# Layer norms moved into the attention stages, first projection weights loaded before the stage that uses them

## The chip, the cores and the metric

The kernel runs on one core of a Trainium2 chip. The metric is device time in microseconds (us), median of three runs.

## The reference, cut to what matters

All arithmetic is float32; x is 16 sequences of 256 tokens and 128 channels.

```python
x = layernorm(x + attention_0(x))      # 16 heads of 8, relative position tables
x = layernorm(x + ffn_0(x))            # itself 6 layers: local attention (16 heads of 64, window 32)
                                       #   and a gated FFN, each with its own residual
x = layernorm(x + attention_1(x))      # 16 heads of 8, causal, over 16 x 256 tokens
x = layernorm(x + moe(x))              # 8 experts, top 2
def layernorm(x): return (x - mean(x)) / sqrt(var(x) + 1e-5)   # over the 128 channels
```

`attention_0` is softmax((q.k + relative terms) / sqrt(8)) times (v + relative values). `ffn_0` multiplies x by Wqkv (128 x 3072) in every layer, normalises and rotates q and k, takes a softmax over a window of 32 keys back, and multiplies by Wo (1024 x 128).

## The kernel before, in words

x lies in SBUF for the whole program as `X` (128 partitions, 32 tiles of 128 channels; a sequence is two tiles). `XR` is a second tensor of that shape. Nothing is scheduled automatically: each engine has a queue that is written out by hand, runs it in order, and waits on semaphores. The program is a row of blocks; an engine enters a block when all have left the one before.

- **Stage A, first attention** (L222 to L898). PE, ScalarE (ACT), VectorE (DVE) and GpSimd (POOL) each run `sequence("first")`, `sequence("loop")` for 15 sequences and `sequence("last")`. PE's products go through a ring of two PSUM banks (`ring_plan`, L99) that ACT and DVE free. DVE writes four groups of outputs per sequence into `XR`; SyncE (SP) stores each with 16 DMAs to a DRAM buffer `oa` (`stores`, L876 to L884), which changes their layout. `q_blk` holds blocks of the queries, which PE reads in `relative_keys`.
- **ln1** (`layer_norm`, L903 to L977). One DMA brings `oa` back into `XR` (L919). DVE adds it to X, takes `bn_stats` and `bn_aggr` over 8 tiles at a time, POOL raises the variance to -0.5 (L968), DVE scales X (L953) and ACT copies X to `XR` (L977), since the residual of the 6-layer part is needed later.
- **Stage B, the 6-layer FFN** (L984 to L1864). A small block loads the rotation tables and masks and lets POOL clear buffers (L1077 to L1102). Then ACT loads Wqkv (1.5 MB, L1577) and splits it in a high part (`high_parts`, L1585) and POOL in a low part (`low_part`, L1235). SP fetches a sequence of X into `xcur` (`fetch_x`, L1202), POOL splits it (`split_x`, L1267 and L1270). Per sequence and layer there are 4 steps; in each PE projects, ACT squares (L1609), DVE rotates (`rotate`, L1740 to L1742), and POOL adds, takes the power and scales (`normalise_rows`, L1241, L1245, L1250). The steps are software pipelined: `one_pass("first")` fills the pipeline, `one_pass("loop")` runs it. SP also copies the values of every step into windows (`windows`, L1149 to L1153).
- **ln2** is `layer_norm` again, without the load and the copy.
- **Stage C, second attention** (L1869 to L2273). A small block loads weights with 14 DMAs, and DVE spreads and scales them (L1916 to L1924). POOL copies a sequence into `xcur` (L1981), PE transposes and projects (L2019), 8 slots per sequence follow, with row maxima on DVE (L2213) and exponentials on ACT (L2169).
- **Stage D, experts** (L2290 on). SP loads the weights with 8 DMAs. The third norm runs per group of 8 tiles: `statistics3` on DVE, `scales3` on POOL, `normalise3` on ACT; PE transposes X (L2404) and computes the gates (L2413).

The 16 stores of a group are issued as

```python
for h in range(8):
    for x in range(2):
        row = 64 * (h // 4) + 32 * x + h % 4 * HD
        sp.dma_start(oa[...], yout[row:row + HD, b * 4 + g, :]...).then_inc(oa_st, 16)
```

Of the kernel before, what the change touches and what calls it, by code (L numbers as in the profile page):

```python
# [25 lines left out]
P = 128  # L26
# [102 lines left out]
def build_program(nc, T, out):  # L129
    ctx = ExitStack()  # L130
    with ctx:
# [27 lines left out]

        x_in = T["L0_attn_x"].rearrange("b (t p) c -> p (b t) c", p=P)  # L160
# [3 lines left out]
        with ExitStack() as st:  # L164
# [21 lines left out]
            q_blk, k_blk = (sb(st, n, [P, H, S]) for n in ("a_q_blk", "a_k_blk"))  # L186
# [13 lines left out]
            yout = XR[:, :, :].rearrange("p t (a c) -> p (t a) c", a=2)  # L200
# [21 lines left out]
            with nc.Block() as block:  # L222
# [119 lines left out]
                def _(pe):  # L342
# [8 lines left out]
                    for i in range(6):  # L351
# [29 lines left out]
            rsum_ok, ysum_ok, yout_ok, oa_st = (sem("a_rsum_ok"), sem("a_ysum_ok"), sem("a_yout_ok"),  # L381
                                                sem("a_oa_st"))
# [7 lines left out]
            with nc.Block() as block:  # L390
                @block.gpsimd
                def _(pool):
                    def sequence(part, b):
# [32 lines left out]
                    with pool.Fori(0, B - 1) as b:  # L426
                        sequence("loop", b)
# [236 lines left out]
                def _(act):  # L664
                    def sequence(part, b):
# [75 lines left out]
                    with act.Fori(0, B - 1) as b:  # L741
                        sequence("loop", b)
                    sequence("last", B - 1)

                @block.vector
                def _(dve):
# [4 lines left out]
                    def sequence(part, b):  # L751
# [85 lines left out]
                        if ahead:  # L837
                            low_parts(qs, q_next, q_low)
                            low_parts(ks, k_parts, k_low)
# [25 lines left out]
                    with dve.Fori(0, B - 1) as b:  # L865
                        sequence("loop", b)
                    sequence("last", B - 1)

                @block.sync
                def _(sp):  # L870
# [5 lines left out]
                    def stores(b, g):  # L876
                        lt, hh = g // 2, g % 2
                        sp.wait_ge(yout_ok, b * 4 + g + 1)
                        for h in range(8):
                            for x in range(2):  # L880
                                row = 64 * (h // 4) + 32 * x + h % 4 * HD
                                sp.dma_start(
                                    oa[b, lt, :, HD * x:HD * x + HD, hh, h, :].rearrange("k l d -> l k d"),
                                    yout[row:row + HD, b * 4 + g, :].rearrange("p (k d) -> p k d", d=HD)  # L884
                                ).then_inc(oa_st, 16)

                    next_x(1)
                    with sp.Fori(0, B - 2) as b:
                        stores(b, 0)
                        stores(b, 1)  # L890
                        next_x(b + 2)
                        stores(b, 2)
                        stores(b, 3)
                    for b in range(B - 2, B):
                        for g in range(4):
                            stores(b, g)

                    sp.wait_ge(oa_st, 16 * B * 4 * 16)  # L898


        def layer_norm(tag, residual, load=None, keep=None, store=None):
            GT = 8
            with ExitStack() as st:  # L903
                stats = sb(st, f"{tag}_stats", [P, 2, GT, 6])
                mv = sb(st, f"{tag}_mv", [P, 2, GT, 2])
                var = sb(st, f"{tag}_var", [P, 2, GT])
# [962 lines left out]
        with ExitStack() as st:  # L1869
# [55 lines left out]

            CS = 4 * LT
# [743 lines left out]
```

## Time and profile before

| | us |
|---|---|
| median of 3 runs | 5302.65 (5301.96 to 5303.74) |
| profiled execution, its own time | 5298.32 |
| its span, first to last instruction | 5296.5 |
| PE busy | 4807.8 (91%) |
| POOL busy | 3431.2 (65%) |
| DVE busy | 3833.2 (72%) |
| ACT busy | 3250.9 (61%) |

The shares are averages over stages with different limits. The program runs stage A to about 1139 us of the span, stage B from 1187 to 4486, stage C from 4510 to 5146 and stage D to the end; the norms lie between. Busy time says nothing of waits, so the stretches between the stages are read from the timeline, which lists instructions in order of time with the idle time of the engine in front of them and what ended it.

### The profile page before, as it was taken

Reading aid. Unit: us, or ns where it says so; the run is one execution under the profiler, and the core shown is the slowest. Engines: PE = TensorE matmul, PEld = TensorE weight load, DVE = VectorE, ACT = ScalarE, POOL = GpSimd, SP = SyncE. Lnnn points to the kernel's source line nnn. Section 1 sums busy time; section 2 is a strip of 40 time slices with the busy share of each in tenths; the row PEclk is TensorE's granted clock in tenths of the full one; section 3 lists DMA queues with packets and bytes.
Section 4 is the critical chain, followed back from the end, with each engine's and each line's share of the span. In section 5 each row is a group of like instructions: output and inputs, shape, how many; then the busy total and the mean of one; then the engine's idle time right before and its main releaser. Section 6 shows DMA issues by size and latency. Waiting matters only on the chain. (4 is left out here: it accounts for less than half of the span.)

```text
span 5296.5 us, 207054 instructions
## 1 busy us (share of the span) xinstructions
PE 4807.8 (91%) x84978; PEld 3972.3 (75%) x84978; DVE 3833.2 (72%) x7728; ACT 3250.9 (61%) x6115; POOL 3431.2 (65%) x2197
## 2 busy tenths in 40 slices
PE   6999999958999999999999999999999997688879
PEld 4888888846887788877887788778877885455557
DVE  4777777756887788877887788778877886444543
ACT  2333333326777777777777777777777774466654
POOL 1111111119999999999999999999999995211212
PEclk8999999988999999999999999999999998888889
DMA  1000000013222322232222322232222221000000
GB/s 44 6 6 6 6 6 6 6 31 87 69 69 67 86 70 68 69 85 69 68 68 72 83 68 68 70 83 68 68 71 72 68 68 38 4 0 0 0 5 17
DMA packets 418744, 253.85 MB, mean 48 GB/s; under 512 B 200864, under 2 KB 414398, under 8 KB 417487
## 3 DMA queue, kind: packets, MB, share of 16 engines
q1 hardware_dynamic: 412464, 235.42, 18.4%
q10 hardware_dynamic: 5920, 12.99, 0.8%
q8 instruction: 304, 4.98, 0.4%
q14 instruction: 56, 0.46, 0.0%
HBM read 25.08 MB, written 4.25 MB: 6 GB/s over the span
## 5 line engine op out<-in xcount | busy, mean ns | idle before, releaser
L1245 POOL TENSOR_TENSOR b_rnorm<-b_ss,neghalf 128x16 f32<-128x16 f32 x384 | 1118.7, 2913 | 35.5 <-DVE b_ss L1753 35.2
L1241 POOL TENSOR_TENSOR b_rot<-b_t 128x1024 f32<-128x1024 f32 x384 | 909.0, 2367 | 96.9 <-DVE b_t L1742 93.6
L1740 DVE TENSOR_TENSOR b_t<-psum,b_cosg 128x1024 f32<-128x1024 f32 x384 | 469.3, 1222 | 483.6 <-ACT b_sq L1609 477.6
L1250 POOL TENSOR_TENSOR b_qk<-b_rot,b_rnorm 128x1024 f32<-128x1024 f32 x384 | 731.5, 1905 | 55.1
L1356 PE MATMUL psum<-b_w_hi,b_xT_parts 128*128 128x512 f32 x1152 | 527.9, 458 | 27.8 <-issue 18.3
L1609 ACT ACTIVATE b_sq<-psum 128x1024 f32<-128x1024 f32 x384 | 392.0, 1021 | 234.6 <-PE psum L1361 234.2
L401 POOL TENSOR_TENSOR a_k_diag<-a_k_parts,a_head_rows 128x1024 fp32r<-128x1024 f32 x64 | 119.9, 1895 | 607.2 <-PE psum L545 565.7
L1747 DVE TENSOR_REDUCE b_ss_floor<-b_sq 128x16 f32<-128x1024 f32 x384 | 463.8, 1208 | 0.0
L1361 PE MATMUL psum<-b_w_hi,b_xT_parts 128*128 128x512 f32 x1152 | 459.3, 399 | 0.7 <-issue 0.7
L1357 PE MATMUL psum<-b_w_lo,b_xT_parts 128*128 128x512 f32 x1152 | 457.8, 397 | 0.0
L1443 PE MATMUL psum<-b_wo,b_oT 128*128 128x128 f32 x3072 | 426.8, 282 | 0.8 <-ACT b_oT L1627 0.8
L1345 PE MATMUL psum<-ident,b_qk 128*128 128x128 f32 x3072 | 404.3, 274 | 15.5 <-DVE b_o L1779 11.9
L1345 PEld LDWEIGHTS psum<-ident,b_qk 128*128 128x128 f32 x3072 | 359.5, 142 | 77.7 <-DVE b_o L1779 21.5
L1987 POOL TENSOR_TENSOR c_k_diag<-c_k_parts,c_head_rows 128x1024 fp32r<-128x1024 f32 x64 | 119.9, 1894 | 454.9 <-DVEq L2233 454.9
L697 ACT ACTIVATE a_probs<-psum,a_nbias 128x256 f32<-128x256 f32 x512 | 195.7, 488 | 347.1 <-DVE a_nbias L769 347.1
L1443 PEld LDWEIGHTS psum<-b_wo,b_oT 128*128 128x128 f32 x3072 | 381.5, 192 | 27.6 <-issue 1.6
L1632 ACT ACTIVATE b_pr<-b_pr 128x512 f32<-128x512 f32 x384 | 241.7, 629 | 207.7 <-DVE b_pr L1763 193.4
L1453 PE MATMUL psum<-b_v_win,b_prT 64*32 64x65 f32 x24576 | 345.0, 225 | 4.2 <-issue 4.0
L1779 DVE TENSOR_TENSOR b_o<-psum,b_rs 128x256 f32<-128x256 f32 x768 | 325.8, 424 | 26.4
L1424 PE MATMUL psum<-b_kT,b_qTs 64*32 64x64 f32 x24576 | 332.5, 224 | 0.0
L1453 PEld LDWEIGHTS psum<-b_v_win,b_prT 64*32 64x32 f32 x24576 | 280.5, 105 | 52.4 <-issue 5.8
L1424 PEld LDWEIGHTS psum<-b_kT,b_qTs 64*32 64x32 f32 x24576 | 269.7, 105 | 65.4 <-issue 65.2
(257 smaller groups left out, 12051.0 us busy)
## 6 DMA issues: line engine op xcount, KB each, us to landing
b_v_win<-b_v SPq DMA_DIRECT2D x2304, 65.0 KB
b_v_win<-b_v SPq DMA_DIRECT2D x1152, 32.5 KB
oa<-XR SPq DMA_DIRECT2D x1024, 2.0 KB
xcur<-X SPq DMA_DIRECT2D x111, 128.0 KB, 4.7
b_wqkv<-in_L_ffn_Wqkv_dram ACTq DMA_DIRECT2D x6, 1536.0 KB
b_x_shifted<-X SPq DMA_DIRECT2D x96, 64.0 KB
b_x_shifted<-X SPq DMA_DIRECT2D x96, 63.5 KB
b_wo<-in_L_ffn_Wo_dram SPq DMA_DIRECT2D x12, 256.0 KB, 3.5
```

Source lines behind the costliest of these rows:

```text
L1241: nc.gpsimd.tensor_tensor(rot[:, i, :, :], t1[:, i, :, :], t2[:, i, :, :], ALU.add).then_inc(rot_done, 1)
L1245: nc.gpsimd.tensor_tensor(rnorm[:, i, :], ss[:, i, :], neghalf[:, :], ALU.pow).then_inc(rn_done, 1)
L1250: nc.gpsimd.tensor_tensor(qk[:, i, :, :], rot[:, i, :, :], rnorm[:, i, :, None].broadcast_to((P, 16, BD)), ALU.mult).then_inc(qk_done, 1)
L1345: last = nc.tensor.transpose(r[:, p * P:(p + 1) * P], qk[:, s % 2, a * 8 + 2 * p:a * 8 + 2 * p + 2, :].rearrange("p h d -> p (h d)"), iden ...
L1356: nc.tensor.matmul(r, xT_hi[:, ts], w_hi[:, piece(hg, i)], start=True, stop=False)
L1357: nc.tensor.matmul(r, xT_hi[:, ts], w_lo[:, piece(hg, i)], start=False, stop=False)
L1361: return nc.tensor.matmul(r, xT_lo[:, ts], w_hi[:, piece(hg, i)], start=False, stop=True)
L1424: last = nc.tensor.matmul(bank[3 + j][qs, p * 2 * WIN:(p + 1) * 2 * WIN], qTs[at, p, qs], kT[at, p, keys], start=False, stop=(p == 3), ski ...
L1443: last = nc.tensor.matmul(bank_c[:, 0:D], oT[:, p, :], wo[:, 4 * (s % SEQ // 2) + p, :], start=(p == 0), stop=(p == 3))
L1453: last = nc.tensor.matmul(r[qs, p * (BD + 1):(p + 1) * (BD + 1)], prT[at, p, qs], v_win[at, s % NV, c, p, :], start=(p == 0), stop=(p == 3 ...
L1740: nc.vector.tensor_tensor(t14, x4, tab(cosg, slice(0, BD), BD), ALU.mult)
L1747: nc.vector.tensor_reduce(ss_floor[:, t, :, 0], sq[:, :].rearrange("p (h d) -> p h d", d=BD), AX.X, ALU.add).then_inc(ss_done, 1)
```

## The change

`layer_norm` is gone.

- **First norm, by sequences.** SP brings sequence n back from `oa` into `XR` after all its stores (`ln_reload`), at the head of sequence n+1. In sequence n+2 DVE adds it to X and takes the moments (`ln_statistics`), POOL makes the scale and shift (`ln_scales`), ACT writes the result to `XR` and to X (`ln_normalise`). So sequences 0 to 13 are normalised within stage A. The last group of stores of sequence 15, its reload and the norms of 14 and 15 stand in stage B, between `one_pass("first")` and `one_pass("loop")`.
- **Projections.** Wqkv and Wo of layer 0 are loaded into `shared`, which is stage A's `q_blk`, by ACT in the last sequence of stage A, when PE has read the last block of queries.
- **Stage B's start.** The small block is gone: DVE clears the buffers within stage B, SP loads q and k gains, tables and masks behind the first `fetch_x`.
- **Second norm** within stage C: sequences 0 and 1 ahead of its first projection, the others two sequences ahead in slots 3 and 11 (DVE) and 4 and 12 (ACT) of the loop. `xcur` is filled after it.
- **Weights of stages C and D** (14 and 8 DMAs) are issued by SP in stage B, between the last two `shift_x`. ACT spreads and scales stage C's weights.
- **Third norm**: statistics of groups 0 and 1, and the scaling of group 0, stand in the last pass of stage C.

```diff
+        shared = sb(ctx, "shared", [P, H * S])
+        def ln_reload(sp, n):
+            if not isinstance(n, int) or n > 0:
+                sp.wait_ge(ln_ld, n * 16)
+                sp.sem_inc(ln_landed, 1)
+            sp.wait_ge(oa_st, (n + 1) * N_OA)
+            sp.dma_start(XR[:, bass.ds(n * LT, LT), :], oa_tiles[:, bass.ds(n * LT, LT), :]).then_inc(ln_ld, 16)
+        def ln_statistics(dve, n):
+            dve.wait_ge(ln_ld, n * 16 + 16)
+            nc.vector.tensor_tensor(tiles, tiles, XR[:, bass.ds(n * LT, LT), :], ALU.add).then_inc(ln_moments, 1)
...
...
+                dve.wait_ge(ln_shift_ok, n)
+            dve.wait_ge(ln_moments, n * LN_STEPS + LN_STEPS)
+            nc.vector.tensor_scalar(ln_var[:, :], mv..., EPS, None, ALU.add).then_inc(ln_var_ok, 1)
+            nc.vector.tensor_scalar(ln_less_mean[:, :], ...).then_inc(ln_var_ok, 1)
+        def ln_scales(pool, n):
+            pool.wait_ge(ln_var_ok, n * 2 + 2)
+                pool.wait_ge(ln_x_ok, n * LT)
+            nc.gpsimd.tensor_tensor(ln_rstd..., ALU.pow).then_inc(ln_rstd_ok, 1)
+            pool.wait_ge(ln_rstd_ok, n + 1)
+            nc.gpsimd.tensor_tensor(ln_shift..., ALU.mult).then_inc(ln_shift_ok, 1)
+        def ln_normalise(act, n):
+            act.wait_ge(ln_shift_ok, n + 1)
+            for t in range(LT):
+                nc.scalar.activation(kept, x, ACT.Identity, bias=..., scale=...)
+                nc.scalar.activation(x, x, ACT.Identity, bias=..., scale=...).then_inc(ln_x_ok, 1)
@@ stage A, DVE and ACT
                         if ahead:
                             low_parts(qs, q_next, q_low)
+                        if norm:
+                            ln_statistics(dve, b - 2)
+                        if ahead:
                             low_parts(ks, k_parts, k_low)
...
                             exps(g, 1, b)
+                            if g == 1 and norm:
+                                ln_normalise(act, b - 2)
+                            if g == 2 and part == "last":
+                                load_projections()
                             turns(g, 0)
@@ stage B, SP
                     fetch_x(0, 0)
-                    load_wo(0, 0)
-                    load_wo(0, 1)
...
+                    fetch_x(0, 1)
+                    stores(sp, B - 1, 3)
+                    ln_reload(sp, B - 1)
                     load_norm(0)
                     load_w1(0)
                     load_w2(0)
-                    fetch_x(0, 1)
                     for s in range(SEQ):
                         windows(0, s)
@@ stage C, DVE
+                            if part == "loop" and j in (3, 11):
+                                statistics(b * 2 + (2 if j == 3 else 3))
+                            if part == "last" and j in (3, 15):
+                                statistics3(dve, j // 15)
```

Three places of the order are shown. The first is POOL at the start of stage B; before, it stood as

```order
L1088 MEMSET b_v 128x2080
L1089 MEMSET b_v_win 128x4160
...
L1267 TENSOR_TENSOR b_x_parts<-xcur,ones 128x256
L1270 TENSOR_TENSOR b_x_parts<-xcur,b_x_parts 128x256
L1278 TENSOR_TENSOR b_cosg<-b_cos,b_qk_gain 128x256
...
L1235 TENSOR_TENSOR b_w_lo<-b_wqkv,b_w_hi 128x512 x6
L1241 TENSOR_TENSOR b_rot<-b_t 128x1024
```

and now

```order
L1376 MEMSET b_ss_floor 128x32
L1337 TENSOR_TENSOR b_x_parts<-xcur,ones 128x256
L1340 TENSOR_TENSOR b_x_parts<-xcur,b_x_parts 128x256
L1305 TENSOR_TENSOR b_w_lo<-shared,b_w_hi 128x512 x2
L1348 TENSOR_TENSOR b_cosg<-b_cos,b_qk_gain 128x256
...
L1305 TENSOR_TENSOR b_w_lo<-shared,b_w_hi 128x512 x4
L1311 TENSOR_TENSOR b_rot<-b_t 128x1024
```

The large clears have gone from POOL, and two of the six low parts stand ahead of the gains.

The second is ACT between the first pass of stage B and its first turn of the loop (`b_xT_parts` is the transposed x of the next sequence, `b_pr` the probabilities, `b_sq` the squares). Before:

```order
L1591 CAST b_xT_parts<-psum 64x512
L1592 CAST b_xT_parts<-psum 64x2x255
L1632 ACTIVATE b_pr<-b_pr 128x512
L1636 COPY psum<-b_masks 128x2x256
L1609 ACTIVATE b_sq<-psum 128x1024
```

and now

```order
L1670 CAST b_xT_parts<-psum 64x2x255
L230 ACTIVATE XR<-X,ln_shift,ln_rstd 128x128
L231 ACTIVATE X<-X,ln_shift,ln_rstd 128x128
L230 ACTIVATE XR<-X,ln_shift,ln_rstd 128x128
L231 ACTIVATE X<-X,ln_shift,ln_rstd 128x128
L230 ACTIVATE XR<-X,ln_shift,ln_rstd 128x128
...
L1710 ACTIVATE b_pr<-b_pr 128x512
L1714 COPY psum<-b_masks 128x2x256
L1687 ACTIVATE b_sq<-psum 128x1024
```

Eight activations, the norms of sequences 14 and 15, stand ahead of the squares on which DVE's next rotation waits. On POOL the matching four instructions stand behind the fourth step of the first pass:

```order
L1320 TENSOR_TENSOR b_qk<-b_rot,b_rnorm 128x1024
L222 TENSOR_TENSOR ln_rstd<-ln_var,neghalf 128x2
L224 TENSOR_TENSOR ln_shift<-ln_less_mean,ln_rstd 128x2
L222 TENSOR_TENSOR ln_rstd<-ln_var,neghalf 128x2
L224 TENSOR_TENSOR ln_shift<-ln_less_mean,ln_rstd 128x2
L1311 TENSOR_TENSOR b_rot<-b_t 128x1024
```

The third place is DVE in the loop of stage A, where the statistics stand between the low parts of the queries and of the keys:

```order
L875 TENSOR_TENSOR a_q_next<-psum,a_q_next 64x512
...
L200 TENSOR_TENSOR X<-X,XR 128x256
...
L214 TENSOR_SCALAR ln_var<-ln_mv 128x2
L215 TENSOR_SCALAR ln_less_mean<-ln_mv 128x2
L871 REGISTER_ALU
L875 TENSOR_TENSOR a_k_parts<-psum,a_k_parts 32x512 x2
```

PE's own order of instructions is the same as before in all stages.

## Rows read from the trace of the kernel before

**Rows 1.** Busy time of engines by stretches; columns as in the first line.
```profile
core 0: us, PE busy (x) PEld busy (x) DVE busy (x) ACT busy (x) POOL busy (x), PEclk, DMA share, GB/s
130.00:1138.70 1008.70, 969.07 (x14658) 850.96 (x14656) 761.41 (x1111) 368.71 (x831) 192.68 (x223) 1.00 0.05 6
...
1156.10:1180.80 24.70, 0.00 (x0) 0.00 (x0) 22.73 (x112) 4.18 (x4) 8.68 (x4) 0.50 0.00 0
...
1187.00:1207.60 20.60, 5.96 (x16) 3.71 (x16) 2.53 (x4) 5.89 (x10) 10.31 (x12) 0.56 0.45 145
...
1238.00:4485.60 3247.60, 3084.69 (x64282) 2585.61 (x64281) 2571.57 (x5529) 2381.66 (x4123) 2990.48 (x1757) 0.99 0.28 71
4485.60:4509.70 24.10, 0.00 (x0) 0.00 (x0) 22.75 (x113) 0.00 (x0) 8.56 (x4) 0.50 0.00 0
...
4521.10:5145.90 624.80, 507.62 (x4158) 343.85 (x4158) 305.34 (x496) 378.61 (x912) 124.97 (x79) 0.89 0.00 0
```

**Rows 2.** Timeline of DVE, start of ln1: start, duration, instruction, [idle before].
```profile
1156.15 1.23 DVE L934 TENSOR_TENSOR X<-X,XR  x1 [17.48 <-DMA XR<-oa]
```

**Rows 3.** Timeline of all engines, start of stage B.
```profile
1187.14 0.54 SPq L1202 DMA_DIRECT2D xcur<-X  x1
...
1194.22 0.61 POOL L1267 TENSOR_TENSOR b_x_parts<-xcur,ones 128x256 fp32r<-128x256 f32 x1 [7.54 <-DMA xcur<-X]
...
1196.63 3.21 ACT L1585 CAST b_w_hi<-b_wqkv 128x512 fp32r<-128x512 f32 x6 [16.09 <-DMA b_qk_gain<-in_L_ffn_k_scale_dram]
...
1198.26 7.43 POOL L1235 TENSOR_TENSOR b_w_lo<-b_wqkv,b_w_hi 128x512 fp32r<-128x512 f32 x6
...
1203.94 1.02 ACT L1609 ACTIVATE b_sq<-psum 128x1024 f32<-128x1024 f32 x1 [3.02 <-PE psum L1361]
...
1205.83 0.62 SPq L1151 DMA_DIRECT2D b_v_win<-b_v  x1
...
1207.57 2.38 POOL L1241 TENSOR_TENSOR b_rot<-b_t 128x1024 f32<-128x1024 f32 x1 [1.88 <-DVE b_t L1742]
```

**Rows 4.** DMA issues of 900 to 1000 us: count, KB each, us to landing.
```profile
xcur<-X SPq DMA_DIRECT2D x1, 128.0 KB, 2.1
```

**Rows 5.** Timeline of ACT and POOL, end of the first pass and the first FFN.
```profile
1227.92 0.58 ACT L1592 CAST b_xT_parts<-psum 64x510 fp32r<-64x510 f32 x1
...
1237.96 2.38 POOL L1241 TENSOR_TENSOR b_rot<-b_t 128x1024 f32<-128x1024 f32 x1
...
1275.94 0.70 POOL L1259 TENSOR_TENSOR b_frstd<-b_fvar,neghalf 128x2 f32<-128x2 f32 x1
...
1277.00 0.88 ACT L1643 ACTIVATE b_xn<-b_x_shifted,b_shift,b_frstd 128x128 f32<-128x128 f32 x2 [5.06 <-POOL b_shift L1261]
```

**Rows 6.** Timeline of DVE and ACT, one sequence of stage A's loop.
```profile
964.19 1.39 DVE L780 TENSOR_TENSOR a_k_parts<-psum,a_k_parts 32x512 fp32r<-32x512 f32 x2 [2.94 <-ACT a_k_parts L678]
...
978.90 1.08 ACT L706 COPY a_probsT<-psum 128x512 f32<-128x512 f32 x2 [5.74 <-PE psum L571]
```

**Rows 7.** Line L882, the stores: duration ns min/median/max, first and last start us.
```profile
L882 SPq DMA_DIRECT2D oa<-XR x1024: 280/283/1368, 126.6 to 1143.9; - x171
```

**Rows 8.** Timeline of ACT, last sequence of stage A.
```profile
1118.89 1.12 ACT L706 COPY a_probsT<-psum 128x512 f32<-128x512 f32 x2
```

**Rows 9.** Timeline of POOL in ln1.
```profile
1160.02 2.65 POOL L968 TENSOR_TENSOR ln_rstd<-ln_var,neghalf 128x8 f32<-128x8 f32 x1 [66.81 <-DVE ln_var L946]
1163.79 1.75 POOL L968 TENSOR_TENSOR ln_rstd<-ln_var,neghalf 128x8 f32<-128x8 f32 x1 [1.12 <-DVE ln_var L946]
```

**Rows 10.** Timeline of SP, end of stage B.
```profile
4439.84 0.77 SPq L1164 DMA_DIRECT2D b_x_shifted<-X  x1
4461.77 0.58 SPq L1161 DMA_DIRECT2D b_x_shifted<-X  x1
```

**Rows 11.** Timeline of PE, first projection of stage C.
```profile
4521.14 2.05 PE L2019 MATMUL psum<-xT,c_wk_rep 128*128 128x256 f32 x4 [0.55 <-ACT xT L2148]
```

**Rows 12.** Timeline of DVE and ACT, slots 4 and 5 in stage C.
```profile
5073.09 1.23 DVE L2213 TENSOR_REDUCE c_nmax<-psum 128x4 f32<-128x1024 f32 x1 [3.37 <-PE psum L2051]
...
5077.37 1.57 ACT L2169 ACTIVATE c_probs<-psum,c_nmax 128x256 f32<-128x256 f32 x4 [0.48 <-DVE c_nmax L2213]
```

**Rows 13.** Timeline of PE, first gates of stage D.
```profile
5158.68 3.58 PE L2413 MATMUL psum<-d_gate_w,d_xT_all 128*128 128x8 f32 x16 [0.68 <-ACT d_xT_all L2500]
```

More of the change, by code:

```diff
@@ L392, in _, with sequence @@
                 def _(pool):
-                    def sequence(part, b):
+                    def sequence(part, b, norm=False):
+                        if norm:
+                            ln_scales(pool, b - 2)
                         for hq in range(NG):
@@ L425, in _ @@
                     sequence("first", 0)
-                    with pool.Fori(0, B - 1) as b:
-                        sequence("loop", b)
+                    sequence("loop", 0)
+                    sequence("loop", 1)
+                    with pool.Fori(2, B - 1) as b:
+                        sequence("loop", b, norm=True)
+                    ln_scales(pool, B - 3)
                 @block.tensor
@@ L664, in _, with sequence @@
                 def _(act):
-                    def sequence(part, b):
+                    def sequence(part, b, norm=False):
                         def take(name):
@@ L749, in _, with sequence @@
                         dve.sem_inc(f, 1)
-                    def sequence(part, b):
+                    def sequence(part, b, norm=False):
                         def take(name):
@@ L864, in _ @@
                     sequence("first", 0)
-                    with dve.Fori(0, B - 1) as b:
-                        sequence("loop", b)
-                    sequence("last", B - 1)
+                    sequence("loop", 0)
+                    sequence("loop", 1)
+                    with dve.Fori(2, B - 1) as b:
+                        sequence("loop", b, norm=True)
+                    sequence("last", B - 1, norm=True)
                 @block.sync
@@ L979, in build_program @@
-        oa_tiles = oa.rearrange("b t k l a h d -> (k l) (b t) (a h d)")
-        layer_norm("ln1", residual=XR, load=oa_tiles, keep=XR)
+                        ln_reload(sp, b - 1)
+                        for g in range(4 if b < B - 1 else 3):
+                            stores(sp, b, g)
+        wqkv_c, wout_c = sb(ctx, "c_wqkv", [P, 3 * D]), sb(ctx, "c_wout", [P, D])
+        wq_rep_c, wk_rep_c = (sb(ctx, n, [P, NG, 4, GC]) for n in ("c_wq_rep", "c_wk_rep"))
+        bias_q, bias_k0, bias_k = (sb(ctx, n, [P, NG]) for n in ("c_bias_q", "c_bias_k0", "c_bias_k"))
@@ new lines, in build_program @@
+        b2 = sb(ctx, "d_b2", [NEXP, D])
+        ROWG = (0, 32)
+        rows = sb(ctx, "d_rows", [ROWG[1] + NEXP, NPR, P])
+        lower = sb(ctx, "d_lower", [P, NEXP, NEXP])
+        stats3, mv3 = sb(ctx, "d_stats3", [P, GD, 6]), sb(ctx, "d_mv3", [P, GD, 2])
+        var3, less_mean3, rstd3, shift3 = (sb(ctx, f"d_{n}3", [P, GD]) for n in ("var", "less_mean", "rstd", "shift"))
+        c_ld2, d_ld = sem("c_ld"), sem("d_ld")
+        N_C, N_D = 14, 8
+        moments3_ok, var3_ok, rstd3_ok, shift3_ok, x3_ok = (
+            sem(f"d_{n}") for n in ("moments3_ok", "var3_ok", "rstd3_ok", "shift3_ok", "x3_ok"))
@@ new lines, in _ @@
+                    nc.gpsimd.memset(mask_all[:, :], -125.0).then_inc(set_c, 1)
+                    scales(0)
+                    copy_x(0)
+                    scales(1)
+                    diagonals(0, 0)
+                    copy_x(1)
+                    with pool.Fori(0, B // 2 - 1) as b:
+                        for q in range(2):
+                            diagonals(b * 2 + 1 + q, 1 - q)
+                            scales(b * 2 + 2 + q)
+                            copy_x(b * 2 + 2 + q)
@@ L2194, in slots @@
                                 prepared(*prepares(part, j + 4))
+                            if part == "loop" and j in (4, 12):
+                                normalised(b * 2 + (2 if j == 4 else 3))
+                            if part == "last" and j in (11, 12, 13, 14):
+                                normalise3(act, 0, range(2 * j - 22, 2 * j - 20))
                     slots("first", 0)
```

481 lines of the change are left out of this document (240 added, 241 removed).

## The prediction

> **What bounds the kernel now.** I read the busy time by stretches first. In stage A PE is busy 969 of 1008.7 us at full clock, in stage B POOL 2990 of 3247.6; in stage C nothing is full, PE 508 of 624.8 [rows 1]. Between the stages the picture turns round: in the 24.7 us of ln1 and the 24.1 us of ln2 only DVE works (22.7 us each), and PE has nothing. So the stages are the bulk, but the gaps between them are what this change can remove. There the timeline says which wait ends last. Stage A's last DVE instruction ends at 1138.70, and DVE then waits 17.48 us for the buffer to come back from DRAM [rows 2]; ln1 takes 24.7; the small block lasts to about 1187; then `xcur`, the weights and the gains are awaited, and the first rotary addition on POOL starts at 1207.57 [rows 3]. From there POOL runs without a break, so this start is the ruler for stage B: what comes earlier there ends earlier. At the other end stage B's last DVE instruction is at 4485.60 and PE's first real projection of stage C at 4521.14 [rows 11]; stage C ends at 5145.90 and the first gates are at 5158.68 [rows 13].
>
> **Stage A to stage B, the start.** In the last sequence ACT issues three DMAs between its exponentials and its copy at 1118.89, which has no idle time before it [rows 8]. An SP issue costs 0.54 [rows 3], I take 0.45 each: 1.3 us later, to 1140.0. The end of the block costs some 0.5 more (the ln2 addition began 0.6 after the stretch cut at 4485.60): stage B starts at 1140.5. SP issues `xcur` in 0.54. Its landing is bounded by 2.1 us in stage A [rows 4] and by 7.1 here, from issue at 1187.14 to its user at 1194.22 beside 1.5 MB of weights [rows 3]. The weights are now issued near 1120 and have 20 us; in the old place they, and all else, were there 9.6 us after the issue at about 1187, so I take the lower end: 1143.1. The two gain DMAs behind it land at about 1144.2. ACT's six casts take 3.21 [rows 3] to 1147.5, its two copies of x 1.2 to 1148.7 (POOL's split of 1.3 and PE's transposes are done by 1146). PE's six matmuls cost ACT a wait of 3.02, squares and rotation 3.63 more (1203.94 to 1207.57) [rows 3]: POOL starts the rotary addition at 1155.4. POOL's own work is earlier: split to 1144.4, low parts at 7.43/6 = 1.24 each [rows 3], tables landed by 1146, gains 1.7, the last four low parts to 1153.6. The gain is 1207.57 - 1155.4 = 52. Were the landings 7 us, it would be 47; at PE's full clock 53. DVE's clears (about 2 us) lie under the landing.
>
> **The norms of sequences 14 and 15 inside the filling pipeline.** This is the added wait that costs. ACT is through with the first pass at 1228.5 [rows 5] (old times here) and now waits for POOL's shift. POOL makes it only after its fourth step, that is at 1237.96 [rows 5]. Then a chain in which each engine waits for the next: POOL 0.70 for the power [rows 5] and 0.25 for the product, to 1238.95; ACT four activations at 0.44 (0.88 for two) [rows 5], to 1240.8; POOL again 0.95, to 1241.8, since `ln_scales` waits for the last normalised tile; ACT four more, to 1243.7. Queued behind them on ACT: exponentials and mask 1.1, then the squares 1.02 [rows 3], to 1245.8. DVE rotates in 2.6, and POOL, which was at work again at 1237.96, goes on at 1248.4. Cost 10.5 us; nothing gives it back, because POOL bounds what follows. Bounds 9 (hops without latency) and 13 (0.4 for each of six hops).
> DVE's two additions fall on POOL's fourth step. The power of L968 took 2.65 us beside DVE's addition of X and XR, 1.75 beside an instruction with one SBUF tensor [rows 9]: 0.9 lost to 1.23 us of addition. Two additions of a quarter of that size cost POOL 0.5. Sum for stage B: 52 - 11 = 41.
> The Trainium skill says this in the GPSIMD Engine Reference, section Key points: GpSimd shares its SBUF interfaces with VectorE and contends with VectorE instructions that read two SBUF inputs. The trace agrees here (2.65 against 1.75). It speaks against the change, since all 32 additions move from where POOL is idle to where it works; by it the sum is 0.5 worse than without it, because stage A's and C's POOL have time.
>
> **SP in stage B.** Ahead of `windows` there now stand 16 stores at 0.28 to 0.5 [rows 7], the wait for their landing, the reload and the FFN's weights. All of the latter were issued between 1187.14 and 1205.83 before [rows 3]; I estimate SP to be free at about 1161 to 1164, 7 to 10 us after the values of step 0 exist (1205.83 - 52 = 1154). PE needs these windows some 21 us after them in the old trace, and the 8 DMAs at 0.62 [rows 3] with a landing of 2 take 7. So 4 us of slack remain, and 0 cost; without it up to 8.
>
> **Inside stage A.** DVE's moments cost about 1.5 us per sequence (22.7/16 = 1.4 in ln1 with its scaling, plus the waits on itself). They are put just where DVE sits 2.94 us waiting for ACT's key parts [rows 6]: hidden. ACT's four activations, 1.8 us, stand ahead of a copy that follows 5.74 us of idle [rows 6]: hidden. POOL idles tens of us. SP's reload waits for the stores of the sequence before, and SP has nothing to do then. PE's order is unchanged. Cost 0; if the cover is short by 1 us, 14.
>
> **Stage B to stage C.** SP has 21 us between the last two `shift_x` [rows 10], and 22 issues of 0.5 are 11: hidden. Stage C starts as ln2 did, at 4486.2. DVE's moments 1.5, to 4487.7; POOL clears `vones` meanwhile, to 4488.2 (ACT's five small conversions too), then 0.95: 4489.2. ACT's two activations 0.88: 4490.1. POOL's copy to `xcur` 0.61: 4490.7, then scales of sequence 1, 1.0; ACT 0.88 and the copy of x 0.4: PE's first projection at 4493.2. Gain 4521.1 - 4493.2 = 28; bounds 24 (a hop of 0.4 at each of nine places) and 29.
>
> **Inside stage C.** DVE's 1.5 us stands before an idle of 3.37: hidden. ACT's 0.88 stands before one of 0.48 [rows 12]: exponentials 0.4 us later, with PE's transposes behind them 1 us late anyway. Cost 0; bounds -3 and 16 x 0.5 = 8.
>
> **Stage C to stage D.** After the last residual (5145.83) DVE takes the moments of group 1, 2.7 us, and POOL its 1.75 for the power [rows 9] and 0.2, to 5150.5; the block ends at 5150.9. The transposes of group 0 no longer wait for its norm: 2.0, copies 0.6, gates at 5153.5 instead of 5158.68 [rows 13]. Gain 5, bounds 3 and 6.
>
> **Sum.** -52 + 10.5 + 0.5 - 28 - 5 = -74. The profiled execution took 5298.3; the median of the runs is 4.3 above it. So 5224 for such an execution, 5228 for the median.
>
> **Rivals.**
> 1. Stage A's cover is short. The statistics have five waits on DVE's own results, each with register work in the loop. For it: DVE has little idle time elsewhere in the sequence. Against: ln1 did the same for eight tiles in about 3.8 us. It decides from 3.2 us per sequence; at 4.5 us it costs 14 x 1.3 = 18: 5246.
> 2. SP is late with the windows in the fill, and ACT and PE wait: 5236.
> 3. The trickle in stage C: the 0.4 us on ACT, and POOL's copy now behind the norm, pass through its one shared PSUM bank: 16 x 0.5 = 8, also 5236.
> 4. Slower than before: nothing inside the stages is hidden, because the two-bank ring of stage A and the one shared bank of stage C hand every delay of DVE or ACT to PE. Price: 14 x (1.5 + 1.8) = 46 and 14 x (1.5 + 0.9) = 34, sum 80 against 74 saved: 5308. It decides from 5.3 us per sequence over both stages. Against it stand the idle times of [rows 6, 12].
> 5. The change does not do what it says: ln1's wait comes back since the weights or the reload of sequence 15 arrive late. The reload has some 25 us from its landing to its use, the weights 20. It would cost the 10 us that a lone weight load took: 5238.
>
> **How the numbers follow.** Forecast 0.60, rival 1 0.10, rival 2 0.10, rival 3 0.10, rival 5 0.05, rival 4 0.02, and 0.03 for more than one of the others. The bounds of the terms are -47 to -53, 9.5 to 14, -24 to -29, -3 to -6 and -3 to 8 for stage C: taken together not all at one end, 5218 to 5242 for the forecast alone. To leave out no more than 2 in 10, with the rivals, I give 5215 to 5252. A measurement of this kernel can tell about 0.2%, 10.6 us, from no change. Faster by more 0.96, within 0.01, slower 0.03.
>
> **What the profile of the changed kernel would show.** POOL's first rotary addition of stage B about 17 us after stage A's last DVE instruction (69 before). A hole of some 10 us on POOL behind the fourth step of the first pass, ended by DVE's rotation. In stage A the same time per sequence and PE as busy; the statistics between the query and the key parts with the wait behind them shrunk from 2.9 to about 1.4. PE's first projection of stage C 7 to 8 us after stage B's last DVE instruction (35.5 before). The gates about 8 after stage C's last residual. The prediction is wrong if stage A or C is longer by over 5 us, or if the hole in the fill is not there.

## The result

The changed kernel takes 5243.41 us in the median (5241.66 to 5245.58, four runs), the kernel before it 5303.19 us on the same chips: ratio 0.9885, 95% interval 0.9868 to 0.9902. So it is 60 us faster, where 75 were forecast. The profiled execution took 5245.58 us with a span of 5243.8; against the profiled execution of before that is 52.7 less, where the sum said 74. The missing 21 us are looked for in the two traces, span against span.

Busy time by stretches in the changed kernel, as in [rows 1]; the cuts are stage A, the fill of stage B, the rest of stage B, the gap to stage C, stage C to the first gates, stage D:

```profile
core 0: us, PE busy (x) PEld busy (x) DVE busy (x) ACT busy (x) POOL busy (x), PEclk, DMA share, GB/s
130.00:1137.60 1007.60, 968.04 (x14646) 850.60 (x14642) 781.60 (x1234) 389.57 (x887) 207.09 (x251) 1.00 0.06 10
1154.80:1195.40 40.60, 21.67 (x276) 15.86 (x284) 22.65 (x47) 17.39 (x32) 31.68 (x19) 0.72 0.22 54
1195.40:4461.70 3266.30, 3094.91 (x64423) 2599.37 (x64423) 2575.51 (x5537) 2381.89 (x4126) 2989.61 (x1757) 0.99 0.29 71
4461.70:4468.70 7.00, 0.69 (x2) 0.29 (x2) 2.68 (x18) 3.64 (x10) 4.29 (x7) 0.50 0.00 1
4468.70:5102.90 634.20, 513.48 (x4166) 347.67 (x4166) 328.41 (x658) 391.80 (x950) 145.63 (x112) 0.88 0.00 0
5102.90:5243.80 140.90, 130.54 (x760) 107.22 (x760) 54.40 (x196) 63.76 (x145) 29.32 (x44) 0.88 0.05 16
```

The stretch 1195.4 to 4461.7 is the one that answers to 1238.0 to 4485.6 in [rows 1]. POOL is busy the same 2990 us in it with the same 1757 instructions, but it is 18.7 us longer. That is the loss, and it isn't work that was added to POOL.

The start of stage B and the place behind the fill, from the timeline (start, duration, engine, line, instruction, [idle before it and what ended it]):

```profile
1140.03 0.61 POOL L1337 TENSOR_TENSOR b_x_parts<-xcur,ones 128x256 fp32r<-128x256 f32 x1 [2.03 <-DMA xcur<-X]
...
1143.47 3.21 ACT L1663 CAST b_w_hi<-shared 128x512 fp32r<-128x512 f32 x6 [11.65 <-DMA b_qk_gain<-in_L_ffn_k_scale_dram]
...
1150.77 1.02 ACT L1687 ACTIVATE b_sq<-psum 128x1024 f32<-128x1024 f32 x1 [3.02 <-PE psum L1439]
...
1154.83 2.38 POOL L1311 TENSOR_TENSOR b_rot<-b_t 128x1024 f32<-128x1024 f32 x1 [1.72 <-DVE b_t L1829]
...
1185.38 0.70 POOL L222 TENSOR_TENSOR ln_rstd<-ln_var,neghalf 128x2 f32<-128x2 f32 x1
...
1186.38 0.49 ACT L230 ACTIVATE XR<-X,ln_shift,ln_rstd 128x128 f32<-128x128 f32 x1 [10.65 <-POOL ln_shift L224]
...
1188.17 0.69 POOL L222 TENSOR_TENSOR ln_rstd<-ln_var,neghalf 128x2 f32<-128x2 f32 x1 [1.82 <-ACT X L231]
...
1192.89 1.23 DVE L1827 TENSOR_TENSOR b_t<-psum,b_cosg 128x1024 f32<-128x1024 f32 x1 [6.28 <-ACT b_sq L1687]
...
1195.39 2.35 POOL L1311 TENSOR_TENSOR b_rot<-b_t 128x1024 f32<-128x1024 f32 x1 [6.26 <-DVE b_t L1829]
```

POOL's first rotary addition is at 1154.83, 52.7 us earlier than in [rows 3] and 17.3 after stage A's last DVE instruction (1137.53). The hole behind the fourth step runs from 1185.38 to 1195.39: 10.0 us, of which 1.8 are work. Both are as forecast. What answers to [rows 11, 13] is PE's first projection of stage C, and the line of the gates (duration ns min/median/max, first and last start):

```profile
4468.74 2.05 PE L2089 MATMUL psum<-xT,c_wk_rep 128*128 128x256 f32 x4 [1.49 <-ACT xT L2220]
```

```profile
L2503 PE MATMUL psum<-d_gate_w,d_xT_all x64: 256/257/379, 5102.9 to 5194.5; 128*128 128x8 f32 x64
```

The projection stands 7.0 us behind stage B's last DVE instruction (4461.70), the gates 634.2 us behind the projection.

**Where the rest went.** I set POOL's 384 steps of the two traces side by side. The lead of the changed kernel is 52.7 us at the first step, 41.2 behind the fill, and then it holds through the passes of a layer and falls at each change of layer: over steps 72 to 84 and the same twelve steps of the next four changes it falls by 1.8, 2.7, 3.2, 4.3 and 2.9 us, 15.0 of the 17.3 that are lost until stage B ends (12.1 at the first four, 2.9 at the fifth). At those places POOL waits for `b_mv`, the moments of the FFN's norm, before L1326. The groups of POOL from 1700 to 4350 us (line, instruction, count, busy and mean, idle before it and what ended it), before:

```profile
L1256 POOL TENSOR_TENSOR b_fvar<-b_mv,b_eps 128x2 f32<-128x2 f32 x79 | 15.6, 197 | 12.8 <-DVE b_mv L1794 12.8
```

and after:

```profile
L1326 POOL TENSOR_TENSOR b_fvar<-b_mv,b_eps 128x2 f32<-128x2 f32 x78 | 15.2, 195 | 25.9 <-DVE b_mv L1881 25.9
```

DVE isn't the cause, it is idle: its moments wait for `b_x_shifted`, which SP brings. At the first change of layer SP's queue reads so, before:

```profile
1838.49 2.83 SPq L1153 DMA_DIRECT2D b_v_win<-b_v  x3
1842.26 0.58 SPq L1161 DMA_DIRECT2D b_x_shifted<-X  x1
```

and after, with DVE's first moments behind it:

```profile
1797.43 2.66 SPq L1190 DMA_DIRECT2D b_v_win<-b_v  x3
1803.66 0.59 SPq L1198 DMA_DIRECT2D b_x_shifted<-X  x1
...
1810.76 0.29 DVE L1875 BATCH_NORM_STATS2 b_st<-b_x_shifted 128x6 f32<-128x128 f32 x1 [7.34 <-issue]
```

Between the last window and the shifted copy SP issues nothing for 0.94 us before, and for 3.57 after (1800.09 to 1803.66). The gap is 3.14, 3.85 and 3.20 at the next three changes (0.92, 0.92, 0.91 before), and 0.53 and 0.54 at the fifth. What sets the four apart from the fifth is in the program: SP's loop over the layers, `sp.Fori(0, DEPTH - 1)`, jumps back to its start there. SP's own instructions in the two traces say where in the gap the time lies: from the end of the taken branch to the next instruction 0.23 to 0.26 us pass before and 2.45 to 3.17 after. The body of that loop is the same before and after: the traces hold 303 instructions of SP for one turn of it, the inner loop counted once. It only begins at another place of SP's program, 69 instructions later by the traces, since the loads and stores ahead of it changed. (The expectations below say 291 instructions and 67 places, from a count of the built program; the traces don't agree with it to the instruction.)

The jump doesn't explain all 15.0 us. At the fifth change nothing jumps back, and 2.9 us are lost all the same. There the 60 transfers that SP issues ahead of the shifted copy took 47.0 us from the first to the last, against 44.0 before; at the other layer changes of all runs with these transfers they took 42.7 to 46.6. So the time that SP needs to issue them varies by some us, and only the 12.1 us of the first four changes can be the jump's, where the gap grew by 10.1 in all.

### The profile page after: what moved, and what is told of

Same layout as the page of the kernel before. It is cut to its first block and busy times, and to the rows that moved or that the text cites. A ratio compares the mean times of both kernels' runs of the same rounds, so it can differ in the third digit from the quotient of the medians.

```text
span 5243.8 us, 207189 instructions
## 1 busy us (share of the span) xinstructions
PE 4819.1 (92%) x84978; PEld 3988.5 (76%) x84978; DVE 3833.0 (73%) x7791; ACT 3281.4 (63%) x6212; POOL 3442.1 (66%) x2250
## 5 line engine op out<-in xcount | busy, mean ns | idle before, releaser
L1521 PE MATMUL psum<-shared,b_oT 128*128 128x128 f32 x3072 | 426.0, 282 | 0.8 <-ACT b_oT L1705 0.8
L1521 PEld LDWEIGHTS psum<-shared,b_oT 128*128 128x128 f32 x3072 | 380.8, 192 | 27.1 <-issue 1.3
L1469 PE MATMUL psum<-ident,b_o 128*128 128x128 f32 x1536 | 242.6, 281 | 86.4 <-ACT b_qTs L1674 83.8
```

Of the source, the lines that this page charges most:

```text
L1521: last = nc.tensor.matmul(bank_c[:, 0:D], oT[:, p, :], wo[:, 4 * (s % SEQ // 2) + p, :], start=(p == 0), stop=(p == 3))
```

## The experiments

All but two start from the changed kernel; its own median is 5243.4, and each ratio is against the kernel before on the same chip. The changed kernel was not timed again beside them: the kernel before was, and its medians lie between 5302.88 and 5305.31. The ratios' intervals are 5 to 9 us to either side. So a difference of 10 us between an experiment and the changed kernel is hardly clear of the noise by the times alone, and the argument rests on the gaps and waits in the traces.

**SP's loop over the layers written out.**

```diff
-                    with sp.Fori(0, DEPTH - 1) as l:
+                    for l in range(DEPTH - 1):
```

> The changed kernel with SP's loop over the layers of stage B written out (four copies of its body; the inner loops over the sequences stay). In the changed kernel the step back from the end of that loop to its start shows as 3.1 to 3.8 us between SP's last window transfer and its first shifted copy (0.9 us before the change), at four of the five layer changes, and POOL then waits 3.7 to 6.0 us for b_mv (1.4 to 4.1 before). Theory 1 (the jump back makes SP late, and SP's lateness is what the layer changes cost): the gap falls to 0.5 to 1.0 us at all four, POOL's waits for b_mv there fall by about 2.5 us each, and the time by 8 to 12 us against the changed kernel: 5232 to 5236. Rival A (SP is late because its queue is full before the jump; the gap only fills slack): the gap goes, POOL's waits fall by under 1 us each, time 5239 to 5244. Rival B (the loss at the layer changes isn't SP's at all): nothing moves, 5242 to 5245.

Measured 5224.91 (5219.16 to 5227.22, five runs), ratio 0.9844 [0.9831, 0.9858]: 18.5 us less than the changed kernel.

```profile
1798.59 1.87 SPq L1190 DMA_DIRECT2D b_v_win<-b_v  x3
1800.83 0.89 SPq L1198 DMA_DIRECT2D b_x_shifted<-X  x1
```

```profile
L1326 POOL TENSOR_TENSOR b_fvar<-b_mv,b_eps 128x2 f32<-128x2 f32 x79 | 15.5, 197 | 6.5 <-DVE b_mv L1881 6.5
```

The gap is 0.37 us at all five changes (the loop runs five times, so it was written out in five copies, not four), and POOL's waits fall from 25.9 to 6.5 us. Theory 1 held, and by more than I gave it: POOL runs from its first rotation to the end of its last step in 3238.3 us against 3259.4. Rivals A and B fell.

**Ten transfers of a layer change given to ACT.**

```diff
-                        if next_ffn:
-                            sp.wait_ge(hid_done, 3 * (n - 1))
-                            load_w1(l)
+                            if j == 0 and new_ffn:
+                                act.wait_ge(hid_done, 3 * (n - 1))
+                                act_load_w1(new_ffn)
```

(W2 and the norm's gain and bias likewise.)

> The changed kernel with ten small transfers of each layer change (the five of W1 and b1, three of W2 and b2, two of the norm's gain and bias) issued by ACT instead of SP. They take SP 5.3 us of issuing in the 40 us ahead of the late shifted copy, in which SP's queue shows no gap over 0.1 us. Theory 1 (SP's queue as a whole bounds the layer change): the shifted copies start some 5 us earlier at all five changes, POOL's waits for b_mv (4.5 to 6.0 us a change, 25.8 in all) fall to under 1.5 us each, and the time by 15 to 22 us: 5222 to 5229. Theory 2 (only the jump back counts): the backlog goes, but the 3 us of the jump stay: 5232 to 5238. Rival (ACT's 4 us of issuing a layer come late on ACT, which squares and normalises for DVE and POOL): what SP gives ACT takes, 5240 to 5250.

Measured 5254.78 (5251.65 to 5267.69), ratio 0.9911 [0.9896, 0.9926]: 11 us more than the changed kernel. The rival held, and the time is 5 us above its range. ACT at the first change of layer:

```profile
1762.83 0.38 ACTq L1652 DMA_DIRECT2D b_b<-in_L_ffn_b_dram  x1
1763.26 0.63 ACT L1721 ACTIVATE b_pr<-b_pr 128x512 f32<-128x512 f32 x1 [5.61 <-issue]
```

ACT's exponentials follow 5.6 us of idle time, in which its queue waits for `hid_done` and issues the transfers, and POOL then waits 5.10 us for the rotation (at 1767.95). The waits for `b_mv` did fall, to 14.9 us in all, but other waits took their place. SP was through with its windows at 1800.03 and issued the shifted copy at 1805.74: its long gap at the jump was still there, so this run says nothing on how much the ten transfers themselves cost.

**The norms of 14 and 15 left out of the fill** (those two sequences go on unnormalised).

```diff
-                    ln_scales(pool, B - 2)
-                    ln_scales(pool, B - 1)
```

(and `ln_statistics` on DVE, `ln_normalise` on ACT.)

> The changed kernel without the norms of sequences 14 and 15 behind the fill of stage B (statistics on DVE, scales on POOL, normalisation on ACT left out, so those two sequences go through the blocks unnormalised); the time shows what the two norms cost on the path. By the trace of the changed kernel POOL stands still 1.82 + 6.26 us there and is busy 1.9 us with the scales, 10.0 us in all. Theory (POOL sets stage B's pace from there on, so its hole is paid in full): 10 to 11 us less than the changed kernel, 5232 to 5234. Rival (what comes later by 10 us at the layer changes makes SP later against POOL, so part is given back): 3 to 7 us less, 5236 to 5241.

Measured 5229.54 (5223.56 to 5232.54), ratio 0.9856 [0.9841, 0.9871]: 13.9 us less. In the trace POOL reaches the fifth step 30.42 us after the first instead of 40.56: the two norms cost 10.1 us there, and the price was paid in full. POOL's waits for `b_mv` stayed at 25.4 us, so the loss at the layer changes doesn't come from the fill. The 4 us on top aren't explained by this part; in the trace stages C and D were 3.2 and 2.9 us shorter than in the changed kernel, and these vary (last section). The rival, that part is given back, fell.

**The second norm as a stage of its own again.**

```diff
+        layer_norm("ln2", residual=XR)
...
-                            statistics(0)
-                            statistics(1)
...
-                            if part == "loop" and j in (3, 11):
-                                statistics(b * 2 + (2 if j == 3 else 3))
```

(and `scales` and `normalised` with them.)

> The changed kernel with the second norm put back as a stage of its own between stages B and C (eight tiles at a time on DVE and POOL, as before the change); the copies of the projections and the loads for C and D stay early. Theory (the norm inside C costs C nothing, and its stage cost about 28 us less the 7 us that C's own first statistics, scales and the wait for them take now): 5243 + 20 to 27, so 5263 to 5270. Rival (the 32 statistics and 32 activations slow stage C by 3 to 8 us, which come back here): 5256 to 5263.

Measured 5262.62 (5250.63 to 5264.7), ratio 0.9912 [0.9898, 0.9926]: 19.2 us more.

```profile
4488.67 0.69 PE L2151 MATMUL psum<-ident,xcur 128*128 128x128 f32 x2 [27.16 <-POOL xcur L2112]
4489.97 2.05 PE L2161 MATMUL psum<-xT,c_wk_rep 128*128 128x256 f32 x4 [0.61 <-ACT xT L2292]
```

PE's first projection of stage C comes 28.0 us after stage B's last DVE instruction, instead of 7.0; from there to the gates it takes 632.6 us instead of 634.2. So keeping the norm out of the gap saves 21 us, and its price inside stage C is 1.6 us in this pair of traces. The pair alone doesn't settle the price, since stage C varies by more than that (last section). Over all runs, from the first projection to the last residual, the eight kernels with the norm inside took 622.9 to 629.7 us and the four without it 623.8 to 625.7; the means are 626.0 and 624.7. That speaks against the rival's 3 to 8 us. The times don't: the median is 0.4 us under the theory's range and inside the rival's.

**The loop moved in SP's program.** The edit puts waits that are long satisfied ahead of the loop. In the built program two such waits share an instruction, so 64 and 128 waits move the loop by 32 and 64 places, not by 64 and 128 as I wrote ahead of the runs.

```diff
+                    for _ in range(64):
+                        sp.wait_ge(x_split, 1)
                     with sp.Fori(0, DEPTH - 1) as l:
```

> The changed kernel with 64 waits that are long satisfied put into SP's program just ahead of its loop over the layers: nothing is computed or moved otherwise, the loop only lies 64 instructions later in the program. In the changed kernel the jump back shows as 3.1 to 3.8 us at four layer changes, before the change as 0.9 us, with the same loop body. Theory P (what the jump costs depends on where the body and its start lie in the program): the gap changes by over 1 us here or with 128 waits, and the time with it, by up to 12 us either way (5232 to 5250). Rival Q (the cost is that of the loop as such and the gap of before was hidden by something else): 3.1 to 3.8 us remain with both, and the time stays within 5240 to 5247.

> As with 64 waits, but 128. Theory P: the gap is another than with 64 or in the changed kernel, 0.5 to 1.5 us in at least one of the two, which then is 6 to 12 us faster than the changed kernel (5231 to 5238). Rival Q: 3.1 to 3.8 us, and 5240 to 5247.

Measured 5234.16 (ratio 0.986 [0.9845, 0.9875]) and 5232.28 (0.9863 [0.9847, 0.9879]), 9 and 11 us less than the changed kernel. The two intervals overlap that of the changed kernel (0.9868 to 0.9902), so the gaps have to decide. With 64 waits:

```profile
1797.48 1.88 SPq L1190 DMA_DIRECT2D b_v_win<-b_v  x3
1800.31 0.73 SPq L1198 DMA_DIRECT2D b_x_shifted<-X  x1
```

The gap is 0.93 to 0.96 us at all four jumps in both, as in the kernel before, and POOL's waits for `b_mv` are 12.0 and 14.4 us. From the taken branch to the next instruction it is 0.25 to 0.28 us. Nothing but the place was changed, apart from the waits themselves: POOL waits 1.1 and 2.9 us once, for `b_mv` at 1268 and 1271 us, which it doesn't in the changed kernel. Theory P held, rival Q fell.

**The kernel before, with its loop moved to where the changed kernel has it.**

```diff
+                    for _ in range(134):
+                        sp.wait_ge(x_split, 1)
                     with sp.Fori(0, DEPTH - 1) as l:
```

> The kernel before the change with 134 long satisfied waits put into SP's program ahead of its loop over the layers. In the built program two of them share an instruction, so the loop lies 67 places later: its first instruction is SP's 521st, exactly where the changed kernel has it (454th before the change; the body is 291 instructions long in both). Theory P (the place of the loop in SP's program sets what the jump back costs): the gap at the jump, 0.92 us in the kernel before, becomes the 3.1 to 3.8 us of the changed kernel, POOL's waits for b_mv at the layer changes grow by 1.5 to 3 us each at four changes, and the time by 6 to 12 us: 5311 to 5317 against 5305. Rival (something else in the changed kernel makes its jump long): the gap stays at 0.9 us and the time within 2 us of 5305.

Measured 5321.2 (5316.68 to 5329.26), ratio 1.0039 [1.0025, 1.0052]: 18 us slower than the kernel before.

```profile
1843.56 1.88 SPq L1153 DMA_DIRECT2D b_v_win<-b_v  x3
1848.66 0.58 SPq L1161 DMA_DIRECT2D b_x_shifted<-X  x1
```

```profile
L1258 POOL TENSOR_TENSOR b_fvar<-b_mv,b_eps 128x2 f32<-128x2 f32 x78 | 15.4, 197 | 21.8 <-DVE b_mv L1796 21.8
```

The gap is 3.22, 3.14, 3.13 and 3.19 us: the loss could be made in the kernel before by the place alone, though by the traces the loop lies 2 instructions short of where the changed kernel has it. The 18 us are 6 more than the 6 to 12 that I gave. 3.0 us of it the waits themselves cost, once, at 1311 us, where POOL waited for `b_mv` in the first FFN; the rest I leave open.

**The changed kernel moved by 256 instructions.**

```diff
+                    for _ in range(512):
+                        sp.wait_ge(yout_ok, 1)
                     with sp.Fori(1, B - 2) as b:
```

> The changed kernel with 256 instructions of satisfied waits (512 waits) early in SP's program, ahead of its loop over the sequences of stage A, so that all that follows lies 256 places later. With 32 and 64 places the gap at the jump back fell from 3.1 to 3.8 us to 0.95 us. Theory P with the block of 256 instructions that the Trainium skill's page NRT Runtime names for the fetch of instructions (section on instruction fetch mechanics): a move by a whole block leaves every jump as it was, so the gap is 3.1 to 3.8 us again and the time that of the changed kernel, 5240 to 5247. Rival (any move helps, or the period is another): 0.9 to 1.0 us as with 32 and 64 places, and 5229 to 5237.

Measured 5239.65 (5236.15 to 5246.56), ratio 0.9881 [0.9866, 0.9896], as the changed kernel. The gap is 3.99, 3.13, 3.51 and 3.91 us, POOL's waits 25.1.

```profile
1799.97 0.60 SPq L1192 DMA_DIRECT2D b_v_win<-b_v  x1
1804.56 0.59 SPq L1200 DMA_DIRECT2D b_x_shifted<-X  x1
```

A move by 256 places changes nothing, while moves by 32, 64 and (from the other kernel) 67 change it by 2 to 3 us a jump. The rival fell. The Trainium skill says in Runtime: NRT & Kernel Launch (the page that the expectation calls NRT Runtime), section Instruction fetch mechanics, that instructions are fetched in blocks of 256, of which an engine holds two, and that a taken branch to a place outside them waits for the block to be fetched. By it a body of 303 instructions lies in two blocks or, in some places, in three, and the jump back costs a fetch at least where it is three. That the place counts and that a move by 256 leaves the gap as it was, the runs show; that the gap is a fetch, and how many blocks the body touched, none of them does.

**The kernel before with its loop written out.**

> The kernel before the change with SP's loop over the layers written out and nothing else. There the jump back shows as 0.92 us of gap and POOL waits 1.4 to 4.1 us for b_mv at the layer changes, 12.8 us in all. With the loop written out the gap of the changed kernel was 0.37 us and the waits 0 to 2.0 us. Theory (the loop costs the kernel before little, as its gap is short, so the changed kernel lost something that before did not have): 2 to 7 us less than before, 5297 to 5302. Rival (the loop costs both kernels alike, some 18 us, and the loss in the changed kernel is a coincidence): 5283 to 5289.

Measured 5298.21 (5290.0 to 5305.73), ratio 0.9985 [0.9976, 0.9994]. The gap falls to 0.36 us and the waits for `b_mv` from 12.8 to 10.1. The theory held, at the end of its range: 7 us less than the 5305.31 of the kernel before beside it. So of the 18.5 us that writing the loop out gives in the changed kernel, some 7 were to be had before the change too, and some 11 are what the change had lost. That agrees with the 12.1 us of the first four layer changes.

**Loop written out and the two norms of the fill apart.**

```diff
                     one_pass(0, -1, ffn=False)
                     ln_scales(pool, B - 2)
-                    ln_scales(pool, B - 1)
                     one_pass(0, 0, ffn=False)
                     one_pass(0, 1)
+                    ln_scales(pool, B - 1)
```

(DVE's statistics of 15 behind pass 1; ACT's normalisation of 14 behind pass 0, of 15 behind pass 2.)

> The changed kernel with SP's loop over the layers written out, and the norms of sequences 14 and 15 apart from each other: statistics of 14 on DVE and its scales on POOL behind the fill as now, its normalisation on ACT a pass later, the statistics and scales of 15 behind pass 1 and its normalisation behind pass 2. POOL's hole of 10.0 us behind the fill was 1.9 us of scales, 1.8 us of waiting for ACT's normalisation of 14 and 6.3 us of waiting for the rotation that DVE began after its statistics of 15, which had waited for POOL. Theory (only the waits between the engines made the hole; apart, each engine finds the other done): the hole shrinks to 1 us of scales and up to 2 us for DVE's statistics, the second place costs as much, so 4 to 8 us less than with the loop written out alone (5224.9): 5217 to 5221. Rival (DVE, which has 0.9 us or less of slack a pass, gives each norm's 2 us on to POOL whole, and ACT its 3.5 us too): under 2 us less, 5223 to 5226.

Measured 5208.0 (5205.84 to 5211.18), ratio 0.9817 [0.9803, 0.983]: faster than both kernels, 35 us under the changed one, 17 under the one with the loop written out alone, and 9 under my range. The rival fell. POOL reaches its fifth step 31.52 us after the first (40.56 in the changed kernel), so 9.0 of the 10 us hole are gone, and the second place costs nothing that shows: from the first rotation to the end of the last step it is 3225.3 us against 3238.3. More than the hole was gained; of the rest, 4.0 us lie elsewhere in stage B, unexplained, and 5.4 and 2.2 in stages C and D, which this edit doesn't touch.

## Why the prediction was right, and where it was not

The time fell in the range, and the sum was 21 us too good. Term by term, span against span:

| step of the prediction | forecast | traces |
|---|---|---|
| start of stage B (rotary addition 1207.57 to 1154.83) | -52 | -52.7 |
| norms of 14 and 15 in the fill, with contention | +11 | +11.5 |
| rest of stage B | 0 | +17.3 |
| stage B to C (35.5 to 7.0 us) | -28 | -28.5 |
| stage C and its end (637.5 to 634.2) | 0 - 5 | -3.4 |
| stage D | 0 | +3.1 |
| sum | -74 | -52.7 |

- **The range**: the time lies in 5215 to 5252, but 1 us above the 5218 to 5242 that the prediction gave for its own chain. The wider range was there for the rivals, and none of them came true; what filled it is a cost that neither the chain nor a rival names. So that the range held is in part luck. (The bounds of the terms, each taken at the same end, add up to 5221 and 5251, so the 5218 lies lower than they reach.)
- **Start of stage B**: held to 1 us, partly since two errors met. The prediction had ACT's three transfers delay its copy by 1.3 us. But ACT's queue issued them from 1114.96 to 1116.36, while its exponentials ran (1114.88 to 1117.90), and the copy followed at once, at 1117.74. Stage A ended at 1137.53, 1.2 us earlier than before. The casts then waited for the gains until 1143.47, 5.9 us behind the end of stage A where 4.2 were forecast. The weights were there.
- **The fill**: the chain was the right one, link by link (POOL, ACT, POOL, ACT, squares, rotation), and leaving the norms out gave back 10.1 us. The next rotation waited another 0.72.
- **Contention**: POOL's rotary addition of the fourth step, beside the first of DVE's two additions, took 2.55 us instead of 2.38. The second addition ran beside the power of that step, which took 2.91 as everywhere. So 0.2, not 0.5; too small to tell.
- **SP late in the fill** (rival 2): SP issued the first window at 1153.72, not at 1161 to 1164, since the 16 stores went out at 0.36 each (5.74 us) and their landing wasn't waited for long. No cost.
- **Inside stage A** (rivals 1 and 4): the wait ahead of the key parts shrank from [rows 6]'s 2.94 to 1.34, as forecast, and a sequence took the same time:

```profile
1027.50 0.16 DVE L215 TENSOR_SCALAR ln_less_mean<-ln_mv 128x2 f32<-128x2 f32 x1
1028.99 1.39 DVE L875 TENSOR_TENSOR a_k_parts<-psum,a_k_parts 32x512 fp32r<-32x512 f32 x2 [1.34 <-ACT a_k_parts L755]
```

- **Rest of stage B**: the step that failed is the sentence of the prediction that what comes earlier at POOL's first rotation ends earlier: "from there POOL runs without a break, so this start is the ruler for stage B". POOL does not run without a break. It stood 12.8 us at the layer changes before, behind an SP queue with no slack there, and the change, which doesn't touch that code, moved it by 69 places in SP's program. That the place made the jump back 2 to 3 us longer, the moves by 32, 64 and 67 show; that cost is 12.1 us of the 17.3. Of the rest, 2.9 lie at the fifth change, where SP took longer to issue, and 2.3 are open. I read SP's queue in the fill and at the end of stage B, where the change edits it, and not where it is fullest.
- **Stages B to C, C, C to D**: held. The two terms for stage C are one line of the table: from the last residual to the gates it is 7.55 us instead of 12.85, so the end gave 5.3 where 5 were forecast, and the stage up to there took 2.0 longer (626.7 against 624.7), which is less than it varies. Rival 3's 8 us don't show.
- **Rival 5** fell: neither weights nor reload were waited for in the fill.

## What to carry to other kernels

An edit ahead of a hardware loop moves the loop's code, and where an engine's queue has no slack at the jump back, that alone can eat a good part of what the edit wins: here 2 to 3 us more at each of four jumps, some 12 us in all. Look in the trace for idle time of a queue right at its loops' jumps, compare it between versions, and write such a loop out where its queue is late (18.5 us here for one line). Where norms are put in a pipeline's fill, don't stack two whose engines wait for each other in turn; a pass apart each finds the other done (9 us of 10).

## What the runs showed of the hardware that I had not expected

**The place of a loop in the program.** The same loop of 303 instructions cost SP 0.91 to 0.96 us or 3.1 to 4.5 us at each jump back, by its place; in the written-out form 0.36 to 0.37.

**Stages C and D vary with the granted clock.** Stage D computes the same in all kernels, and took 137.4 to 148.9 us. In a slice of 20 us the kernel before shows a granted clock of 0.99 where the changed one has 0.82; both are means of the two levels, 1.00 (2.4 GHz) and 0.50 (1.2 GHz):

```profile
5218.70:5238.70 20.00, 19.77 (x128) 16.11 (x127) 7.85 (x25) 11.09 (x28) 6.87 (x10) 0.99 0.05 14
```

```profile
5162.90:5182.90 20.00, 20.00 (x106) 16.39 (x105) 7.61 (x24) 10.09 (x27) 6.96 (x10) 0.82 0.05 14
```

Both slices lie 60 us behind the first gates. PE was busy throughout both; the kernel before did 128 matmuls in its slice, the changed one 106. The kernel with 64 waits had 0.82 over the whole of stage D, and 148.9 us. Stage C took 630.4 to 638.8 us from its first projection to the gates. So some us of difference between two traces may be the clock's in stages C and D, the 3.1 of stage D above among them, and an effect in another stage is better read from that stage's own length than from the whole. Why the clock falls in one kernel and not in the other, at the same point of the stage, no run here tells.
